# Counting edges by bucket and masking their sources: moving a stage of a graph kernel's preparation from VectorE to ScalarE

## What is computed

```python
# layer 0
msgs = edge_val[:, None] * x[edge_col]
agg = segment_sum(msgs, edge_row, num_segments=N_NODES)
out = relu(einsum('ni,oi->no', agg, W))
# layer 1
npj = relu(layer_norm(node_feats @ Wp + bp, gp, betap))
kron = einsum('ea,ek->eak', npj[src], npj[dst]).reshape(En, -1)
kron = relu(layer_norm(kron @ Wk + bk, gk, betak))
kron_feat = segment_sum(kron, dst, num_segments=Vn)
...  # a softmax of edge logits over dst weighs hv[src]; a GRU cell; a last linear layer
```

## Time and profile before

| | us |
|---|---|
| three runs | 9187.38, 9202.79 (median), 9215.1 |
| the profiled execution, its own time | 9201.89 |
| its span in the trace | 9200.4 |
| busy in the span: PE | 6627.9 |
| DVE | 5809.9 |
| ACT | 3779.0 |
| POOL | 4407.1 |
| mean granted clock of TensorE, as a share of full speed | 0.867 |

### The profile page before, as it was taken

How to read it: one execution, slowest core, us unless ns; L and a number is a source line. 1 busy time by engine, 2 the same in 40 slices (tenths; PEclk the granted TensorE clock), 3 DMA queues, 4 the chain that set the end, 5 groups by cost and what they waited for, 6 DMA issues and landing times.

```text
span 9200.4 us, 169831 instructions
## 1 busy us (share of the span) xinstructions
PE 6627.9 (72%) x32823; PEld 4195.6 (46%) x32824; DVE 5809.9 (63%) x16380; ACT 3779.0 (41%) x10923; POOL 4407.1 (48%) x4743
## 2 busy tenths in 40 slices
PE   3253666666666799988877777777777777777898
PEld 2122444444444577733334444444444444444444
DVE  8895444444443566644447777777777777776666
ACT  0000444444444100023336666666666666665333
POOL 0001777777778200000037776776666766674100
PEclk9676777777777999965569999999999999999988
DMA  0002333333322588844467777777777777776200
GB/s 12 0 0 79 100 100 99 99 101 99 99 97 96 194 262 263 262 186 197 192 208 210 205 205 203 204 203 205 200 205 199 207 202 204 203 204 175 64 19 18
DMA packets 973127, 1398.89 MB, mean 152 GB/s; under 512 B 378559, under 2 KB 744498, under 8 KB 959902
## 3 DMA queue, kind: packets, MB, share of 16 engines
q1 hardware_dynamic: 761663, 797.51, 29.0%
q0 software_dynamic: 208448, 596.38, 22.9%
q10 hardware_dynamic: 2586, 1.37, 0.1%
HBM read 986.18 MB, written 415.51 MB: 152 GB/s over the span
## 4 chain that ended last, share of the span: by engine, by line
PE 32%; issue 18%; DVE 16%; DMA 13%; SPq 8%; ACT 7%; POOL 3%; DVEq 1%; ACTq 1%; POOLq 0%
DMA arena_n<-rec_dram 8%; PE ps L1993 7%; SPq L550 7%; PE ps L1890 4%; PE ps L1787 4%; ACT junk L1001 3%; DMA arena_e<-msg_dram 3%; PE ps L2011 3%; PE ps L2002 3%; POOL msg_dram L814 2%; PE ps L1905 2%; DVE arena_r L1305 2%; DVE arena_e L1636 2%; DVE arena_e L1576 2%; ACT L1022 1%
## 5 line engine op out<-in xcount | busy, mean ns | idle before, releaser
L835 POOL DMA_INDIRECT arena_n<-tab_dram,idxs x2624 | 2621.1, 999 | 2756.0 <-DVE idxs L1551 1667.7
L1993 PE MATMUL ps<-arena_n 126*128 126x257 f32 x5232 | 1635.3, 416 | 404.6 <-DVE arena_e L1576 370.3
L814 POOL DMA_INDIRECT msg_dram<-arena_e,idxq x1616 | 1625.6, 1006 | 434.4 <-issue 424.9
L1001 ACT ACTIVATE junk<-ps 128x256 f32<-128x256 f32 x2616 | 995.2, 382 | 1065.8 <-PE ps L1993 937.5
L1879 PE MATMUL ps<-arena_n,arena_r 128*128 x3232 | 1085.1, 494 | 352.9 <-ACT arena_r L902 352.9
L1993 PEld LDWEIGHTS ps<-arena_n 126*128 126x128 f32 x5232 | 868.9, 196 | 910.1 <-DVE arena_e L1576 735.4
L1576 DVE COPY arena_e<-ps 128x257 f32<-128x257 f32 x1962 | 816.5, 422 | 681.7 <-ACT junk L1001 672.9
L1636 DVE SCALAR_TENSOR_TENSOR arena_e<-arena_e,rstd,nbetak_b 128x256 f32<-128x256 f32 x2608 | 1087.4, 481 | 31.6 <-ACT arena_e L1008 18.9
L1879 PEld LDWEIGHTS ps<-arena_n,arena_r 128*128 128x128 f32 x3232 | 753.6, 245 | 592.6 <-issue 466.2
L907 ACT ACTIVATE arena_e<-ps,recq 128x256 f32<-128x256 f32 x1616 | 736.7, 474 | 651.9 <-PE ps L1879 645.7
L1890 PE MATMUL ps<-arena_e,oh 128*128 128x256 f32 x3520 | 816.2, 387 | 88.8 <-DVE oh L1359 88.3
(11 more groups left out here) (335 smaller groups left out, 9115.5 us busy)
## 6 DMA issues: line engine op xcount, KB each, us to landing
arena_n<-m_dram SPq DMA_DIRECT2D x2624, 126.5 KB
arena_e<-msg_dram SPq DMA_DIRECT2D x441, 514.0 KB, 4.5
m_dram<-arena_e SPq DMA_DIRECT2D x49, 1413.5 KB, 4.9
m_dram<-arena_e SPq DMA_DIRECT2D x49, 1285.0 KB, 4.5
arena_n<-tab_dram,idxs POOLq DMA_INDIRECT x2624
hist_dram<-arena_r SPq DMA_DIRECT2D x163, 253.0 KB
arena_n<-rec_dram SPq DMA_DIRECT2D x1616, 2.0 KB
msg_dram<-arena_e,idxq POOLq DMA_INDIRECT x1616
```

The costliest lines, as they stand in the source:

```text
L814: nc.gpsimd.indirect_dma_start(out=msg_dram, in_=msgs[:, u, j, :], in_offset=None, out_offset=bass.IndirectOffsetOnAxis(ap=idxq[:, u, j:j ...
L835: nc.gpsimd.indirect_dma_start(out=feat[:, u, i, :], out_offset=None, in_=tab_dram, in_offset=bass.IndirectOffsetOnAxis(ap=idxs[:, u, i:i ...
L1001: nc.scalar.activation(junk[:, i % 2, 0:D], ps[:, bank_of(i), 1:HC], ACT.Square, scale=1.0 / 16, accum_out=var[:, u % 2, i:i + 1]).then_in ...
L1993: mm(ps[:, bank_of(i), 0:HC], prods_t[0:KM, s % 2, j * P:(j + 1) * P], m_ring[0:KM, i, :], start=True, stop=True).then_inc(e_h, 1)
```

## The change

It does five things.

- VectorE makes the buckets' numbers of all destinations and sources at the start, as float tiles `dst_bk` and `src_bk`.
- **The counts go to ScalarE** (`count_sides`): 100 activations with function Sign, of `bk - b + 0.5`, with the sum over the 1600 edges taken in `accum_out`. The difference of two neighbouring sums, halved, is the bucket's count; VectorE does that for all 50 buckets at once by two instructions on 125 x 50 elements.
- **The masks of the sources go to ScalarE too** (`mask_bucket`): the 50 byte masks no longer come with the counts; ScalarE makes each just ahead of its scan, as floats, by two activations (`Abs` of `bk - b`, then `Relu` of 1 minus it), into one of two buffers. It begins mask b once the product of bucket b - 2 has been counted in `s_prod`.
- VectorE does digits and `map_buckets` of the destinations first; the map of blocks (k = 0) comes after them, and directly ahead of `map_slots`. TensorE's `total_buckets(0)` moves behind the digits' sums.
- SyncE stores the five maps of `map_buckets` first, then the three of k = 0, and only then loads the maps back. The wait for `tile_of` joins a semaphore with others (`s_rowld`).

```diff
-        mask8 = arena_n[0:EP, 0:MASKW].bitcast(U8)
+        mask = [arena_n[0:EP, MASKW - (2 - q) * ET:MASKW - (1 - q) * ET] for q in range(2)]
...
-            def map_edge_tiles():
+            def store_edge_tiles():
...
+            def load_edge_tiles():
+
                 sp.wait_ge(s_mapst, 48 + 80)
...
+            store_edge_tiles()
             for k in range(2):
                 if k == 1:
-                    map_edge_tiles()
+                    load_edge_tiles()
                 sp.wait_ge(s_map, k + 1)
...
+            def count_sides(k, b):
+                past(act, s_side, b + k * NB)
+                nc.scalar.activation(apart, (dst_bk, src_bk)[k], ACT.Sign, bias=at(bk_edge[0:EP, :], b),
+                                     accum_out=at(sides[0:EP, k, :], b)).then_inc(s_side, 1)
+
+            def mask_bucket(b, q):
+                past(act, s_prod, b - 1)
+                act.wait_ge(s_side, b + 2 * NB)
+                step(nc.scalar.activation(apart, src_bk, ACT.Abs, bias=at(bk_no[0:EP, :], b)))
+                nc.scalar.activation(mask[q], apart, ACT.Relu, bias=ones[0:EP, 0:1], scale=-1.0).then_inc(s_side, 1)
+
+            act.wait_ge(s_const, 2)
+            for k in range(2):
+                count_sides(k, 0)
+                with act.Fori(1, NB) as b:
+                    count_sides(k, b)
+            mask_bucket(0, 0)
+            mask_bucket(1, 1)
+            with act.Fori(1, NB // 2) as it:
+                step.loop(0, it, 2)
+                for q in range(2):
+                    mask_bucket(it * 2 + q, q)
...
-            for k, ids in enumerate((dst_i, src_i)):
+            step(ts(bk_no[:, :], iota[:, 0:NB], -1.0, None, ALU.mult))
+            step(ts(bk_edge[:, :], bk_no[:, :], 0.5, None, ALU.add))
+            step(nc.vector.memset(sides[:, :, NB:NB + 1], -float(ET)))
+            for ids, bks in ((dst_i, dst_bk), (src_i, src_bk)):
+                step(ts(bk_i, ids, 7, None, ALU.arith_shift_right))
+                step(nc.vector.tensor_copy(bks, bk_i))
+            dve.sem_inc(s_const, 1)
+            count_buckets()
+            map_buckets()
+            for k in range(2):
                 if k == 1:
-                    count_buckets()
-                    map_buckets()
                     dve.wait_ge(s_mapst, 48 + 80)
                     map_slots()
-
-                step(ts(bk_i, ids, 7, None, ALU.arith_shift_right))
-                step(nc.vector.tensor_copy(bk_f, bk_i))
-                with dve.Fori(0, NB) as b:
-                    ts(at(mask8, b, ET, ET), bk_f, at(iota[0:EP, :], b), 0.0, ALU.is_equal, ALU.add,
-                       accum_out=at(cnt[0:EP, :], b)).then_inc(s_counted, 1)
+                dve.wait_ge(s_side, NB * (k + 1))
+                step(tt(cnt[0:EP, :], sides[0:EP, k, 0:NB], sides[0:EP, k, 1:NB + 1], ALU.subtract))
+                ts(cnt[0:EP, :], cnt[0:EP, :], 0.5, None, ALU.mult).then_inc(s_counted, 1)
...
-                    m = at(mask8, it * 2 + q, ET, ET)
+                    m = mask[q]
+                    dve.wait_ge(s_side, nth(it * 2 + q, 2 * NB))
                     step(nc.vector.tensor_tensor_scan(scan[q], one_row, m, at(base[0:EP, :], it * 2 + q),
                                                       ALU.mult, ALU.add))
...
-            dve.wait_ge(s_rowld, 80)
+            dve.wait_ge(s_rowld, 96)
...
-            total_buckets(0)
             count_digits(0, 0, first=True)
...
             ins.then_inc(s_bsums, 1)
+            total_buckets(0)
             pe.wait_ge(s_spread, 2)
```

More of the change, by code:

```diff
@@ L192, in gnn_program @@
         trow_i = c(MP).bitcast(I32)
+        assert 2 * SC * (LO + HI) + 5 * HI + 10 * BP + 4 * MP <= MASKW - 2 * ET
         c = cutter(arena_n[:, 2 * NA - 2000:])
@@ L234, in gnn_program @@
         w_f, dloc = c(ET)[0:EP], c(ET)[0:EP]
-        src_slot = c(ET)[0:EP]
+        src_slot, src_bk = c(ET)[0:EP], c(ET)[0:EP]
+        dst_bk = prod[1]
+        apart = src_slot
         c = cutter(arena_e)
@@ L274, in gnn_program @@
         cnt, base = sb("cnt", [P, NB]), sb("base", [P, NB])
+        bk_no, bk_edge, sides = sb("bk_no", [P, NB]), sb("bk_edge", [P, NB]), sb("sides", [P, 2, NB + 1])
         tmap_f = sb("tmap_f", [P, NCM])
@@ L321, in gnn_program @@
         s_const, s_wzero = sem("constants_ready"), sem("weights_cleared")
+        s_side = sem("sides_then_masks_ready")
         s_counted, s_totals = sem("buckets_counted"), sem("bucket_totals_ready")
         s_prod, s_psum = sem("slot_product_ready"), sem("slot_product_added")
-        s_map, s_mapst, s_mapld = sem("tile_map_ready"), sem("maps_stored"), sem("tile_map_loaded")
+        s_map, s_mapst = sem("tile_map_ready"), sem("maps_stored")
         s_packed, s_moved, s_flag = (sem(n) for n in (
@@ L515, in _ @@
                 sp.wait_ge(s_mapst, 176)
-                sp.dma_start(tile_of[:, :], map_dram[0:1, :]).then_inc(s_mapld, 16)
+                sp.dma_start(tile_of[:, :], map_dram[0:1, :]).then_inc(s_rowld, 16)
             sp.wait_ge(s_tail, 2)
@@ L542, in _ @@
             sp.dma_start(left, left_dram[0].partition_broadcast(P)).then_inc(s_rowld, 16)
-            sp.wait_ge(s_rowld, 80)
+            sp.wait_ge(s_rowld, 96)
             sp.sem_inc(s_recs, HEAD)
@@ L610, in _ @@
             sp.wait_ge(n_m1, 16 * NT)
-            sp.wait_ge(s_rowld, 96)
+            sp.wait_ge(s_rowld, 112)
             def store_sums(g, u):
@@ L873, in _ @@
                 act.dma_start(dst[:, :], io[L1 + name].partition_broadcast(P)).then_inc(s_wt, 16)
+            def count_sides(k, b):
[18 more added lines that the diff above has]
+                    mask_bucket(it * 2 + q, q)
+            step.loop_ended(0, NB // 2, 2)
             act.wait_ge(s_order, 1)
@@ L1420, in _ @@
             held = step.done
-            dve.wait_ge(s_mapld, 16)
             dve.sem_inc(a_add, HEAD)
@@ L1794, in total_buckets @@
             def total_buckets(k):
-                pe.wait_ge(s_counted, NB * (k + 1))
+                pe.wait_ge(s_counted, k + 1)
                 pe.wait_ge(s_map, k)
@@ L1864, in _ @@
             pe.wait_ge(s_tloc, MP)
-            pe.wait_ge(s_rowld, 80)
+            pe.wait_ge(s_rowld, 96)
             pe.wait_ge(s_x, 32)
@@ L1896, in _ @@
             pe.wait_ge(s_wzero, 1)
-            pe.wait_ge(act_steps, 1)
+            pe.wait_ge(act_steps, NB + 1)
             def m_part(t, u):
```

## The result

The changed kernel took 9154.6 us (median of 4 runs, 9143.1 to 9161.9) against 9202.0 before on the same chip (4 runs): a ratio of 0.9948, 95% interval 0.9929 to 0.9967. It is faster, but it lies 107 us above the forecast of 9048 and 79 above the upper end of its range. The profiled execution took 9161.9 us.

The account below looks back on a forecast made before the run. VectorE's chain until some 795 us was taken as the bound. Removing 180.8 us, less 23.9 for the longer wait and 1.6 added, with 0.3 rounding, gains 155: 9201.9 becomes 9046.9, plus 0.9, forecast 9048, range 9027 to 9076.

Parts of the forecast that it names:

- What is removed: VectorE's preparation: 100 compares over 1600 elements and the start of two loops go, 180.8 us.
- What is added on VectorE: Preparation: buckets' numbers and edges, and two instructions of 125 x 50 for each k, 1.6 us.
- The wait that grows: Ahead of `map_slots`: VectorE stands 38.5 us for stores and loads instead of 14.5, a loss of 23.9 (12.9 to 49).
- factor of 1.81: Single-element stores before the maps' loads: seen landed after 1.81 times their busy stretch, 27.0 us, the value taken.
- the sum of it and a fixed lag: Same stores: busy stretch 14.9 us plus the second trio's 6.2 us, with 21.1 given as the result.
- the count of elements: Same stores: wait scaled by number of elements, 4992 against 1332, 52 us, the upper bound.
- What ScalarE takes: Counts and masks: activation 1.60 us, count 1.95, hundred done at 226, mask 3.5 with waits; all covered, costing nothing.
- rival in which ScalarE paces: Counts and masks: activations of 3.0 us give 9116, of 4.0 give 9316; chance 0.02 slower, 0.01 for 9060 to 9175.
- TensorE at 1.2 GHz: Digits' loop: TensorE, starting earlier, runs at the lower clock, 77 us more, 9125; chance 0.03.
- The sum: Walk through the preparation to the first scan: 350.8 instead of 505.8, a gain of 155.0 us.
- From there on nothing is changed.: From the first scan to the kernel's end: no further change, so the whole 155 us is kept.
- The saving gets lost later: Behind the scans: a clock or DMA state differing by chance eats the gain, no change in time; chance 0.01.

Follow-up runs that it names:

- stores apart: Changed kernel, large stores on their own semaphore, maps' loads before single-element stores, VectorE memset added; with 89 one-element ScalarE copies 9000.9 us, 0.9771.
- ScalarE's loop at 542: Changed kernel with 89 one-element copies on ScalarE ahead of its loops, first kind of chip: 9035.8 us, 0.9806 of the kernel before.
- 10, 40, 70 and 89 copies: One-element ScalarE copies ahead of the loops, in the version with the stores apart: 0.9806, 0.9773, 0.9768 and 0.9771; 89 in the changed kernel: 0.9806.
- the run meant for it: Kernel before with 39 one-element copies on ScalarE ahead of its loops, first kind of chip: 9143.9 us, 0.9932.

## Why the prediction was wrong

**"What is removed", "What is added on VectorE".** Right. The digits start at 30.8 (forecast 30.6), and `map_buckets` ends at 263.9 (267.9); the stretch between is 4 us shorter than I had carried over from before.

**"The wait that grows".** Right in kind, and within 1 us: VectorE waits 37.5 us (38.5). The parts were off in opposite senses: SyncE issues the loads 25.0 us after the first store of single elements (27.0), and they take 12.5 (11.45). The factor of 1.81 between the busy stretch and the release held better than the sum of it and a fixed lag (21.1) or the count of elements (52). In the changed kernel the last packet of these stores ends at 289.1, 10.4 us before the loads are issued; behind the smaller stores of the earlier trace rows the lag was 6.2. That it grows with the stretch rests on these two cases alone. By the Trainium skill, DMA: Bandwidth & Descriptors, "Latency and other measured facts", it would have been an estimated 16.9; the trace has 25.0 for these stores, so that rule is 8 us short here. The stores apart show what the longer wait was worth: the first scan 34 us earlier, and the whole 35 us less.

**"What ScalarE takes".** Right. An activation is 1.63 us (1.60), two counts are 1.87 apart (1.95), and the hundred are done at 216.6 (226). A mask is 3.3 us, the scans' turn the same as before. The rival in which ScalarE paces is out; so is TensorE at 1.2 GHz, since the window over the digits' loop has a granted clock of 0.99.

**The sum.** Up to the first scan it gave a gain of 155; 160 were measured. With ScalarE's loop at 542 the whole kernel took 9036, 12 us from the forecast of 9048. What failed is the sentence behind the sum: **"From there on nothing is changed."** In the code nothing is; in ScalarE's stream, 39 instructions ahead of the loop moved it to a place at which a jump back costs 7.5 us instead of 4.9, 39 times. The sum had put this term at nothing; it measured 115 us in the edge stage, and 121 came back with the copies on ScalarE (3801 to 3680). The rival **"The saving gets lost later"** came nearest. I gave it 0.01 because I looked for chance events in the clock or the DMA, and none for a cause in the change itself.

The profile of before had a sign of it. It has 127.9 us of "issue" ahead of ScalarE's L1001, and 418 packets of code. The Trainium skill, Runtime: NRT & Kernel Launch, section "Instruction fetch mechanics", says that a taken branch to code that is no longer loaded waits for its fetch. With it the 39 instructions would have been a term of unknown sign. The runs agree with that rule, as far as 195 packets fewer and a jump of 0.21 us instead of 4.84 go together. They don't agree on the page's blocks of 16 KiB: by blocks of 256 instructions with two of them loaded, a loop of 382 that is held from some start, and not from the one before it, would be held from the 130 starts behind it too. The loop with 10, 40, 70 and 89 copies lies in these and was fetched again each time, in packets of 8192 bytes.

Shown on the first kind of chip: ScalarE's place makes the loss, VectorE's does not, nor do the tiles' addresses (these also tested by themselves on the other kind). Not shown: the same loss in another kernel, since the run meant for it began one or two instructions behind 453. Argued, with the packets' times in support: that the second standstill is a second piece in sequence, and that the 5 packets a turn which always remain are VectorE's. Open: why on the other kind one instruction on VectorE is worth some 68 us of edge stage, why ScalarE's place is worth nothing there, and what tells the kinds of chip apart.

## What to carry to other kernels

A change ahead of a long loop moves that loop in the instruction streams of its engines, and the cost of the jump back depends on where it then begins: after such a change read "issue" at the loop's first instruction and the count of code packets beside those of before. A loop of some 380 instructions of an engine that paces a stage should be shifted by a few dummy instructions and timed; here 89 of them beside other work were worth 119 us by the medians of two groups of runs (9154.6 to 9035.8), and the version with the stores apart and 40 to 89 copies (8998 to 9001 us, 0.977) beats both kernels. By theory C a single one is the better choice, but that was not timed on the first kind of chip, and on the other kind the shift brought nothing. Where a load needs only some of the stores ahead of it, those belong on a semaphore of their own, with the load issued ahead of stores of single elements.

## What was not expected of the hardware

- Standstills of 4.8 and 2.7 us at a jump back that no semaphore explains, and a loop that loses both by one or two instructions of offset: 418 code packets, nearly all of 8192 bytes, against 223.
- A memset of 0.06 us on VectorE that is worth 72 us on one kind of chip (0.9921 to 0.9851) and nothing on the other (0.9948 to 0.9934, intervals that overlap).
- The same program takes 9202 us on one chip and 11171 to 11384 on others, at a mean granted clock of 0.87 against 0.77 to 0.78. The preparation is equal to the us (first scan at 505.8, and at 505.2 in the kernel before with the three unused tiles on the other kind); the edge stage begins at 4791 against 5318 and takes 3686 against 5154.
